# A chunked scan with its decay exponents made from one 128-row product, and the orders of its engines redrawn

## The reference, cut to what matters

```
dt  = softplus(dt + dt_bias);  Acs = cumsum(dt * A) over the chunk
Ldec[q,s] = exp(Acs[q] - Acs[s]) for s <= q, else 0            (per head)
Y_diag = sum_s (C[q].B[s]) * Ldec[q,s] * (x[s] * dt[s])
states = sum_q B[q] * exp(Acs[-1] - Acs[q]) * (x[q] * dt[q])
Y_off  = C[q] . state_before * exp(Acs[q])
y = (Y_diag + Y_off + D*x) * silu(z);  y = y * rsqrt(mean(y*y) + 1e-5) * rms_w
out = x_in + y @ out_proj_w.T
```

## Time and profile before

| | us |
|---|---|
| median of 3 runs | 2357.78 (2350.35 to 2358.3) |
| profiled execution | 2352.81 |
| its span, first to last instruction | 2351.1 |
| busy in it: PE, DVE, ACT, POOL | 2128.0, 1647.6, 1274.3, 1572.3 |
| granted TensorE clock, mean | 0.944 |

### The profile page before, as it was taken

How to read it: one execution, slowest core, us unless ns; L and a number is a source line. 1 busy time by engine, 2 the same in 40 slices (tenths; PEclk the granted TensorE clock), 3 DMA queues, 4 the chain that set the end, 5 groups by cost and what they waited for, 6 DMA issues and landing times. The chain is left out here.

```text
span 2351.1 us, 40009 instructions
## 1 busy us (share of the span) xinstructions
PE 2128.0 (91%) x11907; PEld 1738.3 (74%) x11907; DVE 1647.6 (70%) x4242; ACT 1274.3 (54%) x2623; POOL 1572.3 (67%) x1599
## 2 busy tenths in 40 slices
PE   4698999898996999999999999999999993799994
PEld 2466666666765888888888888888888882688883
DVE  4768887887756677777877778778777773344444
ACT  3646655665532666666666666666666661233331
POOL 2679888988852666687686776867858675355551
PEclk9989999899987999999999999999999996899996
DMA  1950000000001001010010010100101001455555
GB/s 59 387 193 10 10 10 1 10 1 1 19 1 28 1 1 26 2 39 6 6 39 2 21 24 3 43 1 10 36 1 42 4 7 42 172 193 191 196 174 215
DMA packets 135402, 130.94 MB, mean 56 GB/s; under 512 B 82885, under 2 KB 101359, under 8 KB 135190
## 3 DMA queue, kind: packets, MB, share of 16 engines
q1 hardware_dynamic: 124950, 107.12, 14.9%
q0 software_dynamic: 9088, 17.07, 2.1%
q10 hardware_dynamic: 1152, 4.19, 0.4%
HBM read 64.78 MB, written 65.10 MB: 55 GB/s over the span
## 5 line engine op out<-in xcount | busy, mean ns | idle before, releaser
L1224 POOL TENSOR_TENSOR plo<-pf,phi 128x512 fp32r<-128x512 f32 (+1 forms) x640 | 752.0, 1186 | 339.4 <-ACT phi L1452 306.8
L1450 ACT ACTIVATE pf<-psum 128x512 f32<-128x512 f32 (+1 forms) x640 | 357.1, 558 | 412.9 <-PE psum L1285 308.0
L1452 ACT ACTIVATE phi<-psum 128x512 fp32r<-128x512 f32 (+1 forms) x640 | 355.1, 555 | 0.0
L1596 DVE CUSTOM_DVE_ANT_0 psum<-psum,ahead_wide 128x128 f32<-128x128 f32 (+3 forms) x512 | 246.7, 502 | 69.2 <-PE psum L1338 67.3
L1283 PE MATMUL psum<-phi,x_tok 128*128 128x512 f32 (+1 forms) x640 | 265.8, 415 | 5.8 <-POOL plo L1224 5.8
L1877 POOL DMA_INDIRECT chosen<-yg,xg x156 | 152.8, 979 | 153.2 <-DVE yg L1989 115.1
L1338 PE MATMUL psum<-xT,qT 128*128 128x512 f32 (+3 forms) x768 | 244.5, 346 | 4.8 <-DVE peak L1596 3.3
L1283 PE MATMUL psum<-qT,xT 128*128 128x512 f32 (+1 forms) x640 | 237.9, 372 | 1.9 <-ACT phi L1452 1.3
L1284 PE MATMUL psum<-plo,x_tok 128*128 128x512 f32 (+1 forms) x640 | 237.7, 371 | 0.0
L1285 PE MATMUL psum<-phi,x_tok 128*128 128x512 f32 (+1 forms) x640 | 237.6, 371 | 0.0
L1284 PE MATMUL psum<-qT,xT 128*128 128x512 f32 (+1 forms) x640 | 236.6, 370 | 0.0
(11 more groups left out here) (293 smaller groups left out, 5285.4 us busy)
## 6 DMA issues: line engine op xcount, KB each, us to landing
wg<-turned_w SPq DMA_DIRECT2D x39, 874.0 KB, 4.6
routed<-empty SPq DMA_DIRECT2D x1, 34056.0 KB, 95.9
xg<-routed SPq DMA_DIRECT2D x39, 264.0 KB, 4.2
qT<-nmax SPq DMA_DIRECT2D x512, 0.5 KB, 2.0
y<-chosen SPq DMA_DIRECT2D x8, 1024.0 KB, 10.2
turned_w<-wT SPq DMA_DIRECT2D x8, 874.0 KB, 4.4
x_in_sb<-in_x SPq DMA_DIRECT2D x8, 512.0 KB, 3.4
out<-o_st ACTq DMA_DIRECT2D x8, 512.0 KB, 5.7
```

The costliest lines, as they stand in the source:

```text
L1224: g_.tensor_tensor(plo[:, T % RP, 0:n], pf[:, T % RF, 0:n], phi[:, T % RP, 0:n].bitcast(F32), ALU.subtract).then_inc(a["low_ready"], 1)
L1450: s_.activation(pf[:, T % RF, 0:n], bank[T % RS][:, 0:n], ACT.Exp)
L1452: s_.activation(phi[:, T % RP, 0:n], bank[T % RS][:, 0:n], ACT.Exp).then_inc(a["high_ready"], 1)
L1596: last = v.tensor_tensor_reduce(out=source[:, col:col + n], in0=source[:, col:col + n], in1=ahead_wide[:, HALF - n:HALF], scale=1.0, scala ...
```

## The change

Five things change, all in the scan.

1. The decay exponents take two products of 512 columns per half of the heads: the mask, and `by_key` (weights) times `by_query`. For each chunk and head there are four rows: the sum at the query, its rounding rest, the sum at the key, its rest, so 128 rows cover four chunks and 8 heads. `by_key` is masked to one chunk, `by_query` to one head. Rows of the query kind hold the sum in `by_query` and 1 in `by_key`; rows of the key kind -1 in `by_query`, the sum in `by_key`.
2. The logarithm of the step size is taken off the key's sum, so that the exponential contains dt, and the product of x with dt (`chunk_in` of GpSimd, L328) is gone; `tok` is read directly.
3. The mean square of y and the variance of the layer norm are brought to the power -0.5 together, two columns in one pair of instructions.
4. Added an image: a logarithm, a copy and two scaled copies on ScalarE; one product and two operations for the split on VectorE; four turning products (`turn_sums`) on TensorE; two pairs of products (`spread_sums`) on GpSimd. `tok` and `y1` have three buffers instead of four, `bcs` is put into `thC`, `sum_high`, `sum_part` and `less_log` lie in `xt`.
5. Every engine's order within a step is redrawn, and some pieces move to another step.

```diff
@@ GpSimd
-                    def chunk_in(g):
-                        pool.wait_ge(s["tok_copied"], g + 1)
-                        g_.tensor_tensor(xdt[:, g % 2, :]..., xs3, dt[:, n % 2, c * NH:(c + 1) * NH]..., ALU.mult)
+                    def spread_sums(n, half):
+                        pool.wait_ge(s["sums_set"], n + 1)
+                        need(pool, "seg_ready", (n - 1) * NC + 4 * (half + 1))
+                        g_.tensor_tensor(by_key[:, half, :, :], at_key[:, half, :]..., of_chunk..., ALU.mult)
+                        g_.tensor_tensor(by_query[:, half, :, :], at_query[:, half, :]..., of_head..., ALU.mult).then_inc(s["sums_spread"], 1)
...
                     def chunk_rs(g):
+                        c0, c1 = (1 if g < 0 else 0), (2 if g + 1 < G else 1)
+                        need(pool, "mv_ready", g + 1)
+                            pool.wait_ge(s["ssq_ready"], g + 2)
+                        two = rs2[:, g % 4, c0:c1]
+                        g_.tensor_tensor(two, mv[:, g % 4, 1 + c0:1 + c1], epst..., ALU.add).then_inc(s["ve_ready"], 1)
+                        g_.tensor_tensor(two, two, mhalf..., ALU.pow).then_inc(s["rs2_ready"], 1)
-                    ADDS = {2: range(0, 3), 3: range(3, 6), 4: range(6, 9)}
+                    ADDS = {2: range(0, 3), 3: range(3, 5), 4: range(5, 7), 5: range(7, 9)}
@@ TensorE
+                    def turn_sums(n):
+                        spare_free("sums_low", n + 1)
+                        pe.wait_ge(s["log_less"], n + 1)
+                        for half in range(2):
+                            to = spare[:, half * P:(half + 1) * P]
+                            t.matmul(to, dA[:, 4 * half:4 * half + 4, :, :]..., upto[:, :], start=True, stop=False)
+                            last = t.matmul(to, less_log_flat[:, half, :], ident[:, :], start=False, stop=True)
...
                             t.matmul(seg, ident_bf[:, :], mask_after..., start=True, stop=False)
-                            t.matmul(seg, halves[:, n % 2, :], minus_one..., start=False, stop=False)
-                            last = t.matmul(seg, group_ones..., apart[:, n % 2, :, :], start=False, stop=True)
+                            last = t.matmul(seg, by_key[:, c // 4, c % 4, :], by_query[:, c // 4, 4 * j:4 * j + 4, :], start=False, stop=True)
@@ ScalarE
+                    def log_of_steps(n):
+                        act.wait_ge(s["dA_ready"], n + 1)
+                        a_.activation(log_dt[:, :], dt[:, n % 2, :], ACT.Ln, bias=least[:, 0:1])
+                    def high_sums(n):
+                        act.wait_ge(s["sums_turned"], n + 1)
+                        a_.activation(sum_high.bitcast(F32R), spare[:, 0:2 * P]..., ACT.Copy)
+                    def set_sums(n):
+                        act.wait_ge(s["sums_split"], n + 1)
+                        a_.activation(at_query[:, :, :], sum_part, ACT.Identity, scale=is_query[:, 0:1], bias=not_key[:, 0:1])
+                        a_.activation(at_key[:, :, :], sum_part, ACT.Identity, scale=is_key[:, 0:1], bias=is_query[:, 0:1])
@@ VectorE
+                    def logs(n):
+                        v.tensor_tensor(less_log, log_dt..., minus_key..., ALU.mult)
+                    def split_sums(n):
+                        v.tensor_scalar(sum_part, spare[:, 0:2 * P]..., is_low[:, 0:1], None, ALU.mult)
+                        v.scalar_tensor_tensor(sum_part, sum_high, sign[:, 0:1], sum_part, ALU.mult, ALU.add)
-                    def sums_apart(n):
...
-                    TAPS_AT = {0: ((0, range(0, 4)),), 1: ((0, range(4, 8)),), 2: ((0, range(8, 9)), (1, range(0, 3))),
-                               3: ((1, range(3, 5)),), 4: ((1, range(5, 7)),), 5: ((1, range(7, 9)),)}
+                    TAPS_AT = {0: ((0, range(0, 3)),), 1: ((0, range(3, 6)),), 2: ((0, range(6, 9)),), 3: ((1, range(0, 1)),),
+                               4: ((1, range(1, 4)),), 5: ((1, range(4, 6)),), 6: ((1, range(6, 9)),)}
```

More of the change, by code:

```diff
@@ L788, in _ @@
                                 pad_copy(nn, 1)
+                        if has(n) and j == 6:
+                            tanh_x(n, 1)
                 @block.vector
@@ L970, in _ @@
                                 decays(n)
+                            if j == 7:
+                                gate_z(n, 1)
+                        if has(n - 1) and j == 3:
+                            gate_z(n - 1, 2)
                         if 0 <= step < G:
```

315 lines of the change are left out of this document (165 added, 150 removed).

## The result

The changed kernel takes 2366.22 us (median of 20 runs, 2354.67 to 2379.11), the kernel before 2350.91 (20 runs, 2347.81 to 2387.52): a ratio of 1.005 with an interval of 1.0032 to 1.0068. It is slower by half a per cent, where 2324 was forecast.

What follows compares the result with a forecast made beforehand. No engine filled the time; TensorE and VectorE alternated, and VectorE would bound steps 1 to 6. An image falling from 78.4 to 74.2 us gave 25 over six; with the other images and prologue 31, so 2324, range 2282 to 2354.

Steps and rivals of the forecast that it cites:

- The stalls of TensorE for t and for the normalised input: TensorE's turns of y and of the normalised input waited 3.3 and 2.8 us an image; both waits were to go.
- Last image and prologue: The scan's two ends: 2 us to be gained in the last image, 1 in the prologue (bounds -3 to +3).
- VectorE's own time in the forecast: VectorE's needed time in each step, 7.7 to 9.5 us in steps 1 to 6, said to set their pace.
- 70.8: Image time in us as a sum of steps: VectorE sets steps 1 to 6, TensorE steps 0 and 7.
- Period 74.2: Forecast time in us of an image in full flow, against 78.4 before the change.
- Net +3.0: Price in us an image to VectorE for GpSimd operations running under its taps, raising 70.8 to 73.8.
- 0.4 for this and for windows of half clock: Allowance in us an image for ScalarE's late logarithm and for half clock where TensorE leads.
- rival 2: GpSimd brings Xd late in steps 5 to 7, by 1.8, 3.1 and 2.5 us; 81.2 an image, 2371; chance 0.08.
- the 7.7 for that step: Forecast length in us of step 5 of an image, taken from VectorE's own work in it.
- three operations a step less: The argument against late Xd: GpSimd has three operations fewer in each step.
- Rival 4: Stalls go but half clock stays, in TensorE's steps 7 and 0: 3.3 us an image, 2344 in all; chance 0.10.
- The criterion: The prediction is wrong if VectorE idles more than 6 us an image in steps 1 to 6.

Runs made afterwards that it cites:

- the light kernel: The changed kernel with six of GpSimd's nine tap additions cut to two elements a row (also called the light GpSimd): 2326.3 us, ratio 0.9906 to the kernel before.
- the core order of before: The changed kernel with turn, exponents and output put back in the order of the kernel before, on TensorE and ScalarE: 2401.2 us.

## Why the prediction was wrong, point by point

**The steps that held.** The stalls of TensorE for t and for the normalised input are gone. VectorE is busy for 65.2 us an image (64.7 forecast, before its price for shared access). The spread products take 3.8 us a pair, 7.6 an image (7.5 forecast). GpSimd is busy for 63.2 us (61). TensorE's work fell: the light kernel, at nearly the clock of the kernel before, has it busy for 592 us to the end of the scan and the kernel before for 605; that is 14 us, some of it at another clock, against 25 forecast. Last image and prologue came within 2 us. Steps 1, 2, 4 and 6 took no more than VectorE's own time in the forecast.

**The step that failed.** It is the step from 70.8 to "Period 74.2": "Net +3.0" for shared access on VectorE, "0.4 for this and for windows of half clock", and nothing for TensorE's wait for Xd, which stood apart as rival 2. The runs showed in its place about nothing on VectorE, a wait of TensorE of 3.8 us for Xd in step 5, and half clock in and behind it (11.4 us of the step), which together made 15.9 us of the 7.7 for that step.

1. Shared access. VectorE's taps are not longer than before (1.49 us), the price to it is about nothing. GpSimd pays: its small operations beside taps take 1 to 1.6 us more each. The chain of addition and power that stays was taken as unchanged; it grew by 5.7 us an image. In GpSimd's total that is hidden, as other operations of it got shorter; what counted was that three long cases fell into step 4, ahead of the additions and of the deviation. The prologue's rows had shown both sides stretched (a tap 1.85 and not 1.52, so 0.3 a tap in these rows, and not the 0.5 to 1 of the text), and of the two I priced only VectorE's. No run takes the stretching alone away, so its share in the lateness is argued; that moving the deviation took step 5's waits from 17.0 to 6.2 us and one addition less to 9.1 is measured. The Trainium skill (SBUF — State Buffer, section "Who interferes with whom") says that issue order decides who blocks, and the second waits for the whole of the first. The timeline of step 4 agrees: the 0.18 us operation took 1.23 beside taps of 1.49, and the fade's 1.6 us more is about one tap.
2. Rival 2. It named what happened, a late Xd: in step 5 GpSimd reached it 4.3 us after VectorE's start (369.92 to 374.20), past the rival's 3.5. That its numbers fit, 81.2 us an image and 2371 in all against 81.2 and 2366, is luck. It had 7.4 us of lateness in three steps and no half clock, on top of a price for VectorE that wasn't paid; measured are 5.0 us of waits and the half clock. It had a chance of 0.08 since "three operations a step less" was counted and their length beside taps was not. Its place was wider than the fact: mainly one step (5) and not three.
3. Half clock. 3.83 us of wait don't lengthen a step from 7.7 to 15.9. The other 4.4 are about what the 9.5 us at 1.2 GHz behind the wait lose against the full clock (4.7 by that count). 24 us at half in the image, and 14 before, are 5 us of work more where nothing hides it. The 0.4 was for this. Rival 4 had it in kind and near in size (3.3 us an image), in steps 7 and 0: step 0 has 5.6 us at half in its 12.2 and no wait, step 7 none.

**The criterion.** I had written that VectorE's idling for over 6 us in steps 1 to 6 would refute the bound. In the rows above it is busy for 51.3 of their 58.9 us there, so 7.6 idle: the sign of being wrong that the prediction named came true.

**What stays open.** Two cures are shown, less on GpSimd or shorter products on TensorE. A third thing, more work on TensorE, brings the clock back and no time. Image 6 lost 8.3 of the 12.6 us by which the scan grew, and not by the late Xd: TensorE waits 3.7 us for it there and step 5 takes 7.4. It has the clock at 0.80, where that image had 0.95 before (31 us at half against 7), and the light GpSimd doesn't mend it. Half-rate stretches without a wait before them, there and in step 0, are not explained; that it is the missing columns, A's reading, fits the runs with a third and a fourth product and is not shown for these stretches. No run of the whole kernel both mends the lateness of Xd and gains by it: with the core order of before the waits for it fell to 7.9 us and the time rose.

## What to carry to other kernels

A forecast for three engines at nine tenths has to place each of GpSimd's small operations beside VectorE's or clear of it, step by step, and price it by the longer of the two durations that the trace shows for it; then ask of the first product in TensorE's step whose input comes last. A wait of TensorE of some 4 us is not priced at 4 us: look in the trace at what the clock did in and behind such waits, and add it. And work taken from an engine that isn't the bound in every step is no gain until the waits around it are known; taken from the chain between two engines (here the head products), it makes room for all the rest.

## What the runs showed of the hardware

- TensorE with less work took longer. Without one product of 512 columns in three, the kernel before was granted 0.83 of the full clock from the first chunk to the end of the scan, and with another product in its place 0.89. In the changed kernel, one and two products more took the time at half from 192 to 150 and 124 us, though the waits for Xd stayed (28.3, 24.7 and 24.7 us).
- Half clock often begins in or behind a wait of TensorE, and not always. Step 6 above: 5.5 us idle and 19.2 us at 0.51. The step of 7.3 us with 0.2 us idle was at 1.00, and step 5 with its wait filled had 3 us at half in seven images instead of 61. But in step 0 of the changed kernel the clock fell without a wait. The Trainium skill (TensorE: Matmul & The Clock Gate, section "HAM oscillation — how this bites in real kernels") tells that a pause between bursts of matmuls lets the next burst start at the lower clock. The runs agree in kind, and add the price in a pipeline that doesn't drain: a step with a wait of 3.8 us had 11.4 us at half, some 2 of them in the wait.
- A small GpSimd operation of 0.18 us took 1.23 beside VectorE's taps, a fade 2.16 and not 0.61, while the taps kept their 1.49 us.
- Cutting work on GpSimd made the kernel before slower by 0.5% (1.0049, 1.002 to 1.0078). In its trace two waits of TensorE (2.7 and 2.8 us) stand in one step.
